# The queries' constants for the clip: from one-column products on TensorE to sums on VectorE

## The reference

```python
Q = norm(x) @ Wq + bq;  K = ctx @ Wk + bk;  V = ctx @ Wv + bv     # x (4,256,128), ctx (4,1601,128)
scores = clip(Q @ K.T * scale, -100, 100)
x = x + softmax(scores) @ V
h = norm(x)                                                       # router, top 2 of 8 experts
x = x + sum over the two experts of weight * (down(act(gate_up(h))))
```

```
scale * (xn Wq + bq) . (c Wk + bk)
  = [scale * (xn Wq Wk' + bq Wk')] . c  +  scale * xn . (Wq bk)  +  scale * bq . bk
  =              g . c                  +      q_const           +    row_const
```

## Time and profile before

| what | value |
|---|---|
| median of 3 runs | 156.84 us (156.77 to 156.84) |
| the profiled execution | 156.96 us |
| its span | 155.2 us |
| TensorE busy | 149.2 us, 96% |
| VectorE busy | 103.2 us, 66% |
| ScalarE busy | 100.8 us, 65% |
| GpSimd busy | 49.8 us, 32% |
| one-column products L980 | 16 passes (8 products), 166 to 250 ns each |
| granted TensorE clock | 1.00 in every stretch |

### The profile page before, as it was taken

How to read it: one execution, slowest core, us unless ns; L and a number is a source line. 1 busy time by engine, 2 the same in 40 slices (tenths; PEclk the granted TensorE clock), 3 DMA queues, 4 the chain that set the end, 5 groups by cost and what they waited for, 6 DMA issues and landing times.

```text
span 155.2 us, 3023 instructions
## 1 busy us (share of the span) xinstructions
PE 149.2 (96%) x1004; PEld 136.0 (88%) x1004; DVE 103.2 (66%) x288; ACT 100.8 (65%) x205; POOL 49.8 (32%) x49
## 2 busy tenths in 40 slices
PE   7998799999999999999999999999999999999993
PEld 7988699999999999989988888788888888887892
DVE  0668958386859595963683899957654377552773
ACT  3183878657484736468866656957788677779450
POOL 1356529243505300210067643312333321233020
PEclk9999999999999999999999999999999999999999
DMA  4979999700000000000000000000000000000022
GB/s 116 371 292 404 388 401 384 225 1 4 0 2 0 4 0 0 4 0 2 0 0 4 0 0 0 0 4 0 2 0 0 0 0 0 0 4 0 4 68 68
DMA packets 5909, 10.69 MB, mean 69 GB/s; under 512 B 380, under 2 KB 3080, under 8 KB 5896
## 3 DMA queue, kind: packets, MB, share of 16 engines
q1 hardware_dynamic: 4968, 10.00, 17.9%
q10 hardware_dynamic: 928, 0.53, 1.2%
HBM read 10.00 MB, written 0.52 MB: 68 GB/s over the span
## 4 chain that ended last, share of the span: by engine, by line
PE 78%; DVE 10%; POOL 4%; ACT 3%; issue 3%; DVEq 0%
PE T L1147 14%; PE O L1041 13%; PE S L944 11%; PE S L946 10%; PE S L945 10%; PE T L1025 6%; PE S L951 3%; POOL ex L309 2%; DVE xT L847 2%; DVE up L838 1%; PE S L1147 1%; DVE w_lo L779 1%; DVE sc L631 1%; ACT pr L419 1%; POOL rstd L287 1%
## 5 line engine op out<-in xcount | busy, mean ns | idle before, releaser
L838 DVE TENSOR_SCALAR up<-up 128x512 f32<-128x512 f32 x32 | 13.9, 434 | 24.7 <-ACT up L504 24.7
L350 POOL TENSOR_TENSOR x<-x,xn 128x512 f32<-128x512 f32 x13 | 17.3, 1331 | 38.6 <-ACT xn L524 38.6
L427 ACT ACTIVATE pT<-T 128x512 f32<-128x512 f32 (+1 forms) x32 | 15.4, 513 | 18.4 <-PE T L1025 18.4
L524 ACT ACTIVATE xn<-T,w_scaled 128x128 f32<-128x128 f32 x56 | 16.1, 374 | 17.2 <-PE T L1147 14.1
L944 PE MATMUL S<-x_hi,w_hi 128*128 128x512 f32 x64 | 26.8, 419 | 0.2 <-DVE w_lo L779 0.2
L1041 PE MATMUL O<-pT,ctx_sb 128*128 128x128 f32 (+1 forms) x208 | 25.9, 275 | 0.2 <-ACT pT L427 0.2
L945 PE MATMUL S<-x_lo,w_hi 128*128 128x512 f32 x64 | 25.3, 395 | 0.0
L946 PE MATMUL S<-x_hi,w_lo 128*128 128x512 f32 x64 | 25.3, 395 | 0.0
L1041 PEld LDWEIGHTS O<-pT,ctx_sb 128*128 128x128 f32 (+1 forms) x208 | 24.6, 192 | 0.6 <-ACT pT L427 0.5
L631 DVE TENSOR_SCALAR_CACHE_REDUCE sc<-S,clip_hi 128x400 f32<-128x400 f32 (+1 forms) x32 | 18.9, 630 | 8.7 <-PE S L946 8.5
L498 ACT ACTIVATE keysT_sb<-S,gate_bias 128x512 f32<-128x512 f32 x32 | 22.7, 708 | 1.7 <-PE S L946 1.6
(11 more groups left out here) (127 smaller groups left out, 248.4 us busy)
## 6 DMA issues: line engine op xcount, KB each, us to landing
keysT_sb<-in_ctxT SPq DMA_DIRECT2D x3, 801.0 KB, 9.9
ctx_sb<-in_ctx SPq DMA_DIRECT2D x3, 768.0 KB
gu_sb<-in_gu SPq DMA_DIRECT2D x1, 2048.0 KB, 14.9
ctx_sb<-in_ctx SPq DMA_DIRECT2D x3, 256.0 KB, 4.5
x_sb<-in_x ACTq DMA_DIRECT2D x1, 384.0 KB, 5.0
keysT_sb<-in_ctxT SPq DMA_DIRECT2D x1, 289.0 KB, 5.5
out_x<-xn SPq DMA_DIRECT2D x1, 256.0 KB, 2.3
out_x<-xn SPq DMA_DIRECT2D x2, 128.0 KB, 1.8
```

The source lines that it names most:

```text
L350: nc.gpsimd.tensor_tensor(acc, acc, y_sb[:, k % 2, :], ALU.add).then_inc(y_added, 1)
L524: ins = nc.scalar.activation(y_sb[:, k % 2, t * DIM:(t + 1) * DIM], T[k % 2][:, t * DIM:(t + 1) * DIM], ACT.Copy, scale=w_scaled[:, bass.d ...
L838: nc.vector.tensor_scalar(up[:, k % 2, ih, :], up[:, k % 2, ih, :], 2.0 * LIMIT, 1.0 - LIMIT, ALU.min, ALU.add).then_inc(up_clipped, 1)
```

## The change

qbk is no longer a column but is spread over all partitions as a row of 128: TensorE computes it once in the fold, as a product of bk, broadcast as weights, with wqT, 128 columns. For each tile VectorE then multiplies xn with that row and sums along it, in one tensor_tensor_reduce, which writes the products to xn_scaled and the sum to q_const in SBUF (find_q_const). The one-column products on TensorE are gone, fold_keys is one product. The limits are computed in a function of their own, find_limits, from q_const; limits_ready is given there. fold_sb grows from 131 to 258 columns.

```diff
--- before.py
+++ after.py
@@ -94,9 +94,11 @@
         att_sb = sb("att_sb", [P, 2 * DIM + 2])
         wqT_sb, wkT_sb = att_sb[:, 0:DIM], att_sb[:, DIM:2 * DIM]
         bk_sb, bq_sb = att_sb[:, 2 * DIM:2 * DIM + 1], att_sb[:, 2 * DIM + 1:2 * DIM + 2]
-        fold_sb = sb("fold_sb", [P, DIM + 3])
-        wqk_sb, qbk_sb = fold_sb[:, 0:DIM], fold_sb[:, DIM:DIM + 1]
-        g_bias, row_const = fold_sb[:, DIM + 1:DIM + 2], fold_sb[:, DIM + 2:DIM + 3]
+        fold_sb = sb("fold_sb", [P, 2 * DIM + 2])
+        wqk_sb, qbk_row = fold_sb[:, 0:DIM], fold_sb[:, DIM:2 * DIM]
+        g_bias, row_const = fold_sb[:, 2 * DIM:2 * DIM + 1], fold_sb[:, 2 * DIM + 1:2 * DIM + 2]
+        xn_scaled = sb("xn_scaled", [P, 3, DIM])
+        q_const = sb("q_const", [P, TILES])
         clip_ends = sb("clip_ends", [P, 2])
         more_sb = sb("more_sb", [P, DIM + EXPERTS + EXPERTS * 4])
         wv_sb, wr_sb, gub_sb = more_sb[:, 0:DIM], more_sb[:, DIM:DIM + EXPERTS], more_sb[:, DIM + EXPERTS:]
@@ -203,6 +205,7 @@
         xT_done, xT_copied = sem("xT_done"), sem("xT_copied")
         g_done, g_hi_ready, g_lo_ready = sem("g_done"), sem("g_hi_ready"), sem("g_lo_ready")
         limits_ready = sem("limits_ready")
+        q_product_ready, q_const_ready = sem("q_product_ready"), sem("q_const_ready")
 
         t_done, t_free = [sem("t_done0"), sem("t_done1")], [sem("t_free0"), sem("t_free1")]
         ct_hi_ready, keys_hi_ready, keys_lo_ready = sem("ct_hi_ready"), sem("keys_hi_ready"), sem("keys_lo_ready")
@@ -373,7 +376,7 @@
 
             def copy_fold():
                 act.wait_ge(fold_done, 1)
-                nc.scalar.activation(fold_sb[:], O[:, 0:DIM + 3], ACT.Copy, scale=SCALE).then_inc(fold_ready, 1)
+                nc.scalar.activation(fold_sb[:], O[:, 0:2 * DIM + 2], ACT.Copy, scale=SCALE).then_inc(fold_ready, 1)
 
             def normalise(j):
 
@@ -600,9 +603,13 @@
                 nc.vector.scalar_tensor_tensor(g_lo[:, s], M[:, 0:n * P], g_bias, g_hi[:, s].bitcast(F32),
                                                ALU.add, ALU.subtract).then_inc(g_lo_ready, 1)
 
-                nc.vector.tensor_scalar(clip_hi[:, t0:t0 + n], M[:, 3 * P:3 * P + n], -1.0, clip_ends[:, 0:1],
+            def find_limits(j):
+                t0, n = PREP[j]
+                dve.wait_ge(q_const_ready, j + 1)
+                dve.wait_ge(clip_ends_ready, 1)
+                nc.vector.tensor_scalar(clip_hi[:, t0:t0 + n], q_const[:, t0:t0 + n], -1.0, clip_ends[:, 0:1],
                                         ALU.mult, ALU.add)
-                nc.vector.tensor_scalar(row_max[:, t0:t0 + n, NCH], M[:, 3 * P:3 * P + n], -1.0, clip_ends[:, 1:2],
+                nc.vector.tensor_scalar(row_max[:, t0:t0 + n, NCH], q_const[:, t0:t0 + n], -1.0, clip_ends[:, 1:2],
                                         ALU.mult, ALU.add).then_inc(limits_ready, 1)
 
             def split_ctx(g):
@@ -612,6 +619,17 @@
                 dve.wait_ge(ct_hi_ready, g + 1)
                 nc.vector.tensor_tensor(ct_lo[0][:, s], T[g % 2][:, 0:w], ct_hi[0][:, s].bitcast(F32),
                                         ALU.subtract).then_inc(t_free[g % 2], 1)
+
+            def find_q_const(j):
+
+                t0, n = PREP[j]
+                if j == 0:
+                    dve.wait_ge(fold_ready, 1)
+                dve.wait_ge(xn_ready, j + 1)
+                for t in range(n):
+                    ins = nc.vector.tensor_tensor_reduce(xn_scaled[:, t, :], xn[:, t0 + t, :], qbk_row, 1.0, 0.0, ALU.mult,
+                                                         ALU.add, q_const[:, t0 + t:t0 + t + 1])
+                ins.then_inc(q_const_ready, 1)
 
             def find_clip_ends():
 
@@ -788,17 +806,20 @@
             moments(x_sb, stats, mv, ve, 0, TPB, var_ready)
             normalise(xn, x_sb, mv, rstd, 0, TPB, rstd_ready, 1, xn_ready)
             find_clip_ends()
+            find_q_const(0)
             dve.wait_ge(x1_in, 16)
             moments(x_sb, stats, mv, ve, *PREP[1], var_ready, neg_mean)
             split_ctx(0)
-            dve.wait_ge(clip_ends_ready, 1)
             split_g(0)
+            find_limits(0)
             split_ctx(1)
             clip_scores(0)
             finish_scores(0)
             clip_scores(1)
             finish_scores(1)
             split_g(1)
+            find_q_const(1)
+            find_limits(1)
             moments(x_sb, stats, mv, ve, *PREP[2], var_ready, neg_mean)
             clip_scores(2)
             finish_scores(2)
@@ -812,6 +833,8 @@
                 invert_sums(b)
                 if b == 0:
                     split_g(2)
+                    find_q_const(2)
+                    find_limits(2)
                 clip_scores(n, [0, 1, 2])
                 residual(b)
                 clip_scores(n, [3])
@@ -964,9 +987,10 @@
             def fold_weights():
 
                 pe.wait_ge(att_in, 16)
-                nc.tensor.matmul(O[:, 0:DIM + 1], wqT_sb, att_sb[:, DIM:2 * DIM + 1], start=True, stop=True)
-                nc.tensor.matmul(O[:, DIM + 1:DIM + 2], wkT_sb, bq_sb, start=True, stop=True)
-                nc.tensor.matmul(O[:, DIM + 2:DIM + 3], bq_sb.to_broadcast([P, P]), bk_sb, start=True,
+                nc.tensor.matmul(O[:, 0:DIM], wqT_sb, wkT_sb, start=True, stop=True)
+                nc.tensor.matmul(O[:, DIM:2 * DIM], bk_sb.to_broadcast([P, P]), wqT_sb, start=True, stop=True)
+                nc.tensor.matmul(O[:, 2 * DIM:2 * DIM + 1], wkT_sb, bq_sb, start=True, stop=True)
+                nc.tensor.matmul(O[:, 2 * DIM + 1:2 * DIM + 2], bq_sb.to_broadcast([P, P]), bk_sb, start=True,
                                  stop=True).then_inc(fold_done, 1)
 
             def fold_keys(j):
@@ -975,11 +999,7 @@
                 if j == 0:
                     pe.wait_ge(fold_ready, 1)
                 pe.wait_ge(xT_copied, j + 1)
-                nc.tensor.matmul(M[:, 0:n * P], wqk_sb, xT[:, t0 * P:(t0 + n) * P], start=True, stop=True)
-                for t in range(n):
-                    ins = nc.tensor.matmul(M[:, 3 * P + t:3 * P + t + 1], xT[:, (t0 + t) * P:(t0 + t + 1) * P],
-                                           qbk_sb, start=True, stop=True)
-                ins.then_inc(g_done, 1)
+                nc.tensor.matmul(M[:, 0:n * P], wqk_sb, xT[:, t0 * P:(t0 + n) * P], start=True, stop=True).then_inc(g_done, 1)
 
             def transpose_ctx(g):
                 t0, n = CTX_GROUPS[g]
```

## The result

The changed kernel takes 159.25 us (median of 4, 158.59 to 159.84) against 156.81 (median of 4); the ratio is 1.0152, 95% interval 1.0102 to 1.0203. It is slower by 2.4 us, where 1.7 had been forecast, on a median that lies between two levels: two of its runs are at 158.6 and 158.7, two at 159.8. The profiled execution is one of the lower level: 158.73, span 157.0, 1.8 us longer than before. The forecast's terms are for this level; experiments 7 to 10 look for the cause of the upper one. The forecast's range was 157.0 to 159.2: the lower level lies inside it, the median on its upper end (0.05 above), the upper level outside.

A forecast was written before the change was run, and what follows sets the result against it. TensorE, busy 96%, was taken to bound the kernel, VectorE counting only where TensorE waits for it. Terms -0.14 + 0.81 - 0.56 + 0.82 + 0.7 gave +1.6; 156.96 + 1.6 - 0.12 = 158.5 us, range 157.0 to 159.2.

The forecast's parts named there:

- GpSimd in the way: Third preparation: GpSimd's two key subtractions meet VectorE's second and third products and hold VectorE, about +0.7 us.
- second stall: Third preparation: three VectorE products between g_lo and limits delay project_v, +0.82 us, plus +0.7 for GpSimd's hold.
- start: Fold and first preparation: extra fp32 product +0.21, four one-column passes gone -0.35, together -0.14 us.
- first stall: Second preparation: three VectorE products delay ScalarE's xn, so TensorE waits before tile 1's weighted sum; +0.81 us in the sum.
- the extra product adds 0.43 before that point: Fold: extra product costs 0.43 before loads double pace; warm-up loads give 0.21 back, leaving +0.21 at the transposes.
- Third preparation's passes: TensorE at about 30 us: the one-column passes on the chain disappear, -0.56 us.
- second preparation's passes: TensorE: six one-column passes, hidden behind the wait at 17.84 for tile 0's exponentials, worth 0.
- A product on VectorE: Each new VectorE product with accumulator takes 0.27 us, bounds 0.13 and 0.41; three take 0.82.
- (b): Rival, 8%: two fp32 SBUF inputs run at half pace with an accumulator, product 0.41, total 159.3 us.
- could be twice that: Third preparation: GpSimd's second subtraction could double the +0.7 us hold on VectorE.
- idle for 1.5 us before project_v: Third preparation: TensorE's wait before project_v would be about 1.5 us instead of 0.23.

The follow-up runs named there:

- experiments 7 to 10: Changed kernel executed once each for two traces (159.78, 159.60 us), with nine products of zeros filling TensorE's idle time (158.77 us), and run again unaltered (158.79 us).
- e11: Kernel before plus only the fold's additional product, bk broadcast with wqT, into spare columns: 156.69 us, ratio 0.9998.
- e6: Changed kernel with second and third preparations' VectorE products moved ahead of split_g, and find_limits ahead of it in all three: 155.57 us, ratio 0.9933.
- e9: Changed kernel with nine products of zeros on TensorE in its idle time before project_v(0): 158.77 us, ratio 1.0114 to the kernel before.
- e5: Kernel before without the one-column products and nothing in their place, limits from a constant tile: 155.51 us, ratio 0.9934.
- e4: Changed kernel, but GpSimd waits for the third preparation's limits before keys_lo(2, 1): 157.48 us, ratio 1.0045 to the kernel before.
- e7: Changed kernel unaltered, one more execution for a trace of its upper level: 159.78 us.
- e2: Changed kernel with only find_q_const(1), the second preparation's products, moved ahead of split_g(1): 157.87 us, ratio 1.0080 to the kernel before.

## Why the prediction was right, step by step

The mechanism was right: two places where TensorE waits for VectorE's new products, and GpSimd in the way at the second. The sum for the profiled execution was +1.6, the spans say +1.8. Part of that agreement is luck: the second stall was 0.45 longer than forecast, and the start and the first stall together 0.25 better.

1. Start, -0.14 forecast, -0.32 in the trace. From the first transposes to the third score chunk the kernel before takes 5.32 (6.78 to 12.10), the changed kernel 4.88 (6.90 to 11.78): the four passes were worth 0.44, not 0.35. The transposes themselves are 0.12 later, not 0.21, and that is not the extra product: TensorE waits there for xn, whose moments begin at 4.37 instead of 4.11, when x has landed. The step "the extra product adds 0.43 before that point" took one profile's pace for the kernel's. In the 11 traces with fold and extra product the loads reach the fast pace anywhere from 4.3 us (e11) to 6.2 or later (e6, e9), and in 8 of them a wait of 0.28 to 1.05 stands before the first transposes. In e6 and e9, where the slow pace lasts, the loads and not xn set the first transposes (7.30 and 7.25), so there the extra product can cost; how much, no run shows.

2. Third preparation's passes, -0.56: between the start of tile 1's sum and g_hi the changed kernel gains 0.42 + 0.14 = 0.56. That the second preparation's passes were hidden holds too (e5).

3. A product on VectorE: 0.27 taken, 0.21 measured, inside the bounds of 0.13 and 0.41. (b) is out: at half pace 128 columns alone would take 2 x 128 x 0.00104 = 0.27. The Trainium skill's rule (Vector Engine (DVE) Microarchitecture Reference, "7. Points that are easy to get wrong") does not carry over to this instruction: measured 0.21 from start to start, the accumulator read out under the next.

4. First stall, 0.81 forecast, 0.42 + 0.32 = 0.74 measured; three products and the wait for their semaphore make 0.76, less the slack of about 0.03.

5. Second stall, 0.82 + 0.7 forecast, 1.97 measured (2.84 less 0.87). The products and waits are 0.76 again, the third product's hold 0.70 as forecast. What the prediction left at "could be twice that" is clip_hi's 0.52: GpSimd's second subtraction held the next VectorE instruction too. I had looked for a partner with two tensor inputs in SBUF and had taken the limits' new source, SBUF for PSUM, for a small gain. In the kernel before, the limits were nearly done when GpSimd began (row_max from 32.26 to 32.47, GpSimd from 32.41), and the clips behind them, which read PSUM, kept their length under it. What can be held had been there to see 5 us earlier. Kernel before, then the changed kernel:

```profile
27.39 0.87 DVE L806 TENSOR_SCALAR gate_bias<-more_sb 128x32 f32<-128x32 f32 x1
...
28.26 0.16 DVE L808 CAST wr_hi<-more_sb 128x8 fp32r<-128x8 f32 x1
...
32.39 0.62 DVE L631 TENSOR_SCALAR_CACHE_REDUCE sc<-S,clip_hi 128x400 f32<-128x400 f32 x1
```

```profile
27.84 0.86 DVE L829 CAST wr_hi<-more_sb 128x8 fp32r<-128x8 f32 x1
```

gate_bias has one SBUF tensor as input and takes 0.87 under GpSimd's subtractions of 25.71 to 28.21, where up_bias behind it, of the same shape, takes 0.17. So one input in SBUF is enough to be held. That limits from bank M would have kept their length under GpSimd is argued from the clips; no run has them there.

6. The clock was not among the rivals. The forecast had TensorE idle for 1.5 us before project_v and looked at the end of that wait only, not at the pace of what follows it. The fall of the clock costs 1.2 us in half of the changed kernel's runs and makes most of the 0.75 by which the median lies above the forecast; the lower level is 0.16 above it. It doesn't change the sign.

## What to carry to other kernels

Moving work from a full engine to one with idle time pays only if it goes into the idle time: with six of the eight sums behind g_lo the kernel is 2.4 us slower than before, with the same six ahead of it 1.0 faster. When an operand moves from PSUM to SBUF, look at what GpSimd does in that stretch: here it made a product of 0.28 us 0.98 long and clip_hi, 0.23 otherwise, 0.74. And a stall on TensorE can cost more than its length: here 2.31 us idle cost 1.2 us more in half of the runs.

## What the runs showed of the hardware

- GpSimd's subtraction of two SBUF tiles also holds a VectorE instruction on three columns with one SBUF tensor and an SBUF scalar: 0.74 for 0.23 (changed kernel and e4). In the changed kernel a cast of eight columns at 27.84, under another such subtraction, took 0.86 where it had been 0.16; in the kernel before gate_bias, 32 columns, took 0.87 for up_bias's 0.17. A clip of 400 columns that reads PSUM took 0.62 under such a subtraction (kernel before, 32.39), as with GpSimd idle (changed kernel, 34.21).
- A tensor_tensor_reduce of 128 fp32 columns from SBUF is 0.28 to 0.29 long and starts every 0.21.
- Behind 2.31 us without work TensorE's granted clock can fall to the lower level: 1.00 through the idle time and up to 35.0, 0.50 from 35.5 to 38.5 (e7), in 6 of 12 executions of the changed kernel and 2 of 9 of e2. With 1.11 us of idle time (e4) none of seven executions shows it.
